# Node update of a two-layer graph network: x laid out for 6 and 8 KB pieces, one operand read from PSUM, and the pairwise additions moved to GpSimd

## The reference, cut to what matters

```
u_s  = x_s Lu_s + sum over (p, q) of Wu_ss[p, q, :] * x_s[p] * a_s[q]
                + sum over (p, q) of Wu_vv[p, q, :] * (x_v[p] . a_v[q])
u_v  = x_v Lu_v + sum over (p, q) of Wu_sv[p, q, :] * x_s[p] * a_v[q]
                + sum over (p, q) of Wu_vs[p, q, :] * x_v[p] * a_s[q]
```

## Time and profile before

| | |
|---|---|
| median of 3 runs | 14576.01 us (14514.0 to 14614.86) |
| profiled execution, its own time | 14720.34 us |
| its span | 14718.6 us |
| PE, PEld, DVE, ACT, POOL busy in the span | 75%, 52%, 58%, 33%, 57% |
| `node_update0` in the span | about 4372 to 6505 us |

### The profile page before, as it was taken

How to read it: one execution, slowest core, us unless ns; L and a number is a source line. 1 busy time by engine, 2 the same in 40 slices (tenths; PEclk the granted TensorE clock), 3 DMA queues, 4 the chain that set the end, 5 groups by cost and what they waited for, 6 DMA issues and landing times. The chain is left out here.

```text
span 14718.6 us, 198660 instructions
## 1 busy us (share of the span) xinstructions
PE 11062.6 (75%) x42082; PEld 7618.9 (52%) x42082; DVE 8564.2 (58%) x16029; ACT 4894.4 (33%) x9080; POOL 8450.8 (57%) x7876
## 2 busy tenths in 40 slices
PE   0168888888879999967787878888788787853777
PEld 0034444444432222227777777777777777741444
DVE  6316666666659999975555555555555555532332
ACT  0026666666651111112232333333323333311333
POOL 0327888788779999975554555555555555534000
PEclk9959999999989999986666666666666666655555
DMA  2127777777779999962222322223322323221000
GB/s 113 39 101 151 154 154 154 152 156 154 154 146 218 218 220 219 219 147 77 86 86 84 89 88 88 87 85 90 89 85 88 89 86 90 89 61 39 13 13 13
DMA packets 1237597, 1650.64 MB, mean 112 GB/s; under 512 B 215337, under 2 KB 865917, under 8 KB 1207261
## 3 DMA queue, kind: packets, MB, share of 16 engines
q1 hardware_dynamic: 841700, 1188.34, 29.6%
q0 software_dynamic: 395520, 458.93, 17.8%
HBM read 1472.37 MB, written 443.97 MB: 130 GB/s over the span
## 5 line engine op out<-in xcount | busy, mean ns | idle before, releaser
L461 POOL DMA_INDIRECT sums<-e_total,e_place x1568 | 2483.3, 1584 | 460.1 <-issue 419.0
L1842 POOL DMA_INDIRECT e_rows<-TS,e_at x1568 | 1624.7, 1036 | 464.1 <-issue 420.9
L1842 POOL DMA_INDIRECT e_rows<-TD,e_at x1568 | 1511.0, 964 | 477.6 <-issue 477.6
L2012 PE MATMUL ps<-e_val,e_q 128*128 128x168 f32 x3136 | 1055.7, 488 | 828.0 <-DVE e_val L1915 516.6
L2026 PEld LDWEIGHTS ps<-w_lv,e_dT 128*128 128x128 f32 x9408 | 1571.9, 245 | 0.0
L2026 PE MATMUL ps<-w_lv,e_dT 128*128 128x32 f32 x9408 | 1525.4, 306 | 0.0
L1897 DVE TENSOR_TENSOR e_silu<-e_silu,w_ad 128x256 f32<-128x256 f32 x392 | 166.6, 425 | 2315.2 <-ACT e_val L2120 1971.3
L598 PE MATMUL ps<-e_win,e_pick 128*128 128x448 f32 x3136 | 1348.4, 576 | 204.4 <-DVE e_u L495 152.9
L129 POOL TENSOR_TENSOR e_gather_cell<-zeros 1x1 f32<-1x1 f32 x392 | 186.2, 475 | 2244.4 <-DVE e_m L1854 2114.6
L2012 PEld LDWEIGHTS ps<-e_val,e_q 128*128 128x128 f32 x3136 | 803.2, 314 | 973.7 <-issue 932.3
L1990 PE MATMUL ps<-w_r,e_h 65*128 65x224 f32 x3136 | 1149.7, 537 | 129.0 <-issue 59.8
(11 more groups left out here) (392 smaller groups left out, 21971.2 us busy)
## 6 DMA issues: line engine op xcount, KB each, us to landing
e_win<-T SPq DMA_DIRECT2D x1568, 168.0 KB
n_z<-in_x_columns SPq DMA_DIRECT2D x400, 512.0 KB
n_zv<-in_x_columns SPq DMA_DIRECT2D x800, 192.0 KB
TOT<-e_tot SPq DMA_DIRECT2D x392, 352.0 KB
e_row<-in_src_rows SPq DMA_DIRECT2D x98, 1024.0 KB
e_row<-in_dst_rows SPq DMA_DIRECT2D x98, 1024.0 KB
e_win<-T SPq DMA_DIRECT2D x1568, 56.0 KB
e_local<-LR SPq DMA_DIRECT2D x98, 512.0 KB
```

The source lines that it names most:

```text
L461: pool.indirect_dma_start(sums[c], bass.IndirectOffsetOnAxis(ap=place[:, p, c:c + 1], axis=0), total[:, p, c, 0:MSG0], None, compute_op=AL ...
L1842: pool.indirect_dma_start(rows[:, p, x, c, :], None, table, bass.IndirectOffsetOnAxis(ap=at[:, gp, x, col:col + 1], axis=0)).then_inc(rows ...
L2012: last = pe.matmul(tot2[:, c % 2], q[:, j % 2, c, :], val[:, slot // 4, 4 * (slot % 4) + c, :], start=True, stop=True)
```

## The change

It does four things, all in `node_update0` and in what the host hands over:

1. The host adds two arrays with the values of x in another order: `in_x_scalar_rows` (four rows of 512 side by side) and `in_x_vector_rows` (the three components of one vector side by side). `z` is then loaded in pieces of 8 KB, `zv` and `xst` in pieces of 6 KB. The bytes are the same.
2. `scalars` on VectorE reads the stacked sums from PSUM bank A1 in place of `a0`. `a0` keeps 64 partitions. Since A1 is in use to the end of a group, `stack0` and `keep0` of the next group go to the end of the group (step 7), and the three `stack1` all use bank A0.
3. `pair` goes from VectorE to GpSimd, behind `vectors` of the same part. `p2` gets a second buffer and `mixed` no longer waits for `paired`.
4. `zv` has two buffers in place of four; `load_zv` goes to the end of SyncE's step, behind `load_x`, `load_sums` and `store`.

```diff
-        four, agT, a0 = sb("n1_four", [128, GW]), sb("n1_agT", [V3, GW]), sb("n1_a0", [128, 2, GW])
-        z, zv = sb("n1_z", [128, 4, 4, GW]), sb("n1_zv", [128, 4, 3, GW])
-        p1, p2 = sb("n1_p1", [128, 2, 3, GW]), sb("n1_p2", [128, 3, GW])
+        four, agT, a0 = sb("n1_four", [128, GW]), sb("n1_agT", [V3, GW]), sb("n1_a0", [S, 2, GW])
+        z, zv = sb("n1_z", [128, 4, 4, GW]), sb("n1_zv", [128, 2, 3, GW])
+        p1, p2 = sb("n1_p1", [128, 2, 3, GW]), sb("n1_p2", [128, 2, 3, GW])
...
                     for j in range(2):
-                        sp.dma_start(z[S * j:S * j + S, s % 4],
-                                     xT[8 * s + j:8 * s + 8:2, at].unsqueeze(0).broadcast_to([S, 4, GW])
+                        sp.dma_start(z[S * j:S * j + S, s % 4].rearrange("v k n -> v (k n)"),
+                                     xz[at, s, j].rearrange("g k n -> g (k n)").broadcast_to([S, 4 * GW])
                                      ).then_inc(z_here[s % 4], 16)
...
                 def load_zv(g, s):
-                    if not (g.before(1) and s < 4):
+                    if not (g.before(1) and s < 2):
                         gate(sp, k)
-                        sp.wait_ge(zv_used, g.n(8, s - 3))
+                        sp.wait_ge(zv_used, g.n(8, s - 1))
...
                         if ahead[0].within():
                             load_z(*ahead)
-                            load_zv(*ahead)
                         if s == 1 and g.plus(1).within():
                             load_x(g.plus(1))
                         if s == 3 and g.plus(2).within():
                             load_sums(g.plus(2))
                         if s >= 6 and not g.before(1):
                             store(g.plus(-1), s - 6)
+                        if ahead[0].within():
+                            load_zv(*ahead)
...
+                def pair(g, s):
+
+                    gate(pool, k)
+                    pool.wait_ge(weighed, g.n(16, 2 * s + 2))
+                    pool.tensor_tensor(p1[:, s % 2], p1[:, s % 2], p2[:, s % 2], ALU.add).then_inc(paired, 1)
+
                 def body(g):
                     for s in range(PARTS):
                         vectors(g, s)
+                        pair(g, s)
...
-                    dve.tensor_tensor(z[:, s % 4], z[:, s % 4], bc(a0[:, g.p, :], 4, 1), ALU.mult).then_inc(z_ready, 1)
+                    dve.tensor_tensor(z[:, s % 4], z[:, s % 4], bc(ps[:, A1, :], 4, 1), ALU.mult).then_inc(z_ready, 1)
...
                     dve.wait_ge(g_up, g.n(16, 2 * s + 2))
-                    if not (g.before(1) and s == 0):
-                        gate(dve, k)
-                        dve.wait_ge(paired, g.n(8, s))
-                    dve.tensor_tensor(p2[:], bc(ps[:, G2, :], 3, 1), xst[:, g.p], ALU.mult).then_inc(weighed, 1)
-
-                def pair(g, s):
-                    gate(dve, k)
-                    dve.wait_ge(weighed, g.n(16, 2 * s + 2))
-                    dve.tensor_tensor(p1[:, s % 2], p1[:, s % 2], p2[:], ALU.add).then_inc(paired, 1)
+                    dve.tensor_tensor(p2[:, s % 2], bc(ps[:, G2, :], 3, 1), xst[:, g.p], ALU.mult).then_inc(weighed, 1)
...
                 def stack0(g):
                     gate(pe, k)
                     pe.wait_ge(ag_kept, g.n(1, 1))
+                    if not g.before(1):
+                        gate(pe, k)
+                        pe.wait_ge(z_ready, g.n(8))
                     pe.matmul(ps[:, A1, :], W["stack"][:], agT[:], start=True, stop=True).then_inc(a0_up, 1)
...
-                            if s == 3:
+                            if s in (3, 4, 5):
+                                stack1(b, s - 3)
+                            if s == 7:
                                 stack0(b)
-                                stack1(b, 0)
-                            if s in (4, 5):
-                                stack1(b, s - 3)
                         pick(g, s)
```

More of the change, by code:

```diff
@@ L971, in groups, with node_update0 @@
         body(Group(0, 0).plus(i))
-def node_update0(nc, m, k, ps, W, xT, sums, X1, TS, TD):
+def node_update0(nc, m, k, ps, W, xT, xz, xw, sums, X1, TS, TD):
     own = ExitStack()
@@ L992, in node_update0 @@
         x_here, ag_here = [sem(f"n1_x_here{p}") for p in range(2)], sem("n1_ag_here")
-        z_here, zv_here = ([sem(f"n1_{n}_here{b}") for b in range(4)] for n in ("z", "zv"))
+        z_here, zv_here = ([sem(f"n1_{n}_here{b}") for b in range(count)] for n, count in (("z", 4), ("zv", 2)))
         stored = [sem(f"n1_stored{r}") for r in range(2)]
@@ L1100, in vectors @@
                 def vectors(g, s):
-                    b = s % 4
+                    b = s % 2
                     gate(pool, k)
-                    pool.wait_ge(zv_here[b], g.n(128, 64 * (s // 4) + 64))
+                    pool.wait_ge(zv_here[b], g.n(256, 64 * (s // 2) + 64))
                     if s == 0:
@@ L1203, in body @@
                             norm2(c)
-                        pair(g, s)
                         if s + 1 < PARTS:
@@ L1245, in stack1 @@
                         e = slice(R * j, R * j + R)
-                        last = pe.transpose(ps[:, (A0, A1, A0)[i], e], four[:, e], I[:])
+                        last = pe.transpose(ps[:, A0, e], four[:, e], I[:])
                     last.then_inc(a1_up, 1)
@@ L1263, in maps @@
                         pe.wait_ge(weighed, g.n(16, 2 * s))
-                    pe.matmul(ps[:, G2, :], W["uvs"][:, 128 * s:128 * s + 128], a0[0:S, g.p, :], start=True, stop=True
+                    pe.matmul(ps[:, G2, :], W["uvs"][:, 128 * s:128 * s + 128], a0[:, g.p, :], start=True, stop=True
                               ).then_inc(g_up, 1)
@@ L1284, in outer @@
                     pe.wait_ge(zv_ready, g.n(24, 3 * s + 3))
-                    pe.matmul(ps[0:S, U0, :], W["uvv"][:, s, :], zv[:, s % 4, 0, :], start=False, stop=s == 7
+                    pe.matmul(ps[0:S, U0, :], W["uvv"][:, s, :], zv[:, s % 2, 0, :], start=False, stop=s == 7
                               ).then_inc(zv_used, 1)
@@ L1375, in _ @@
                 turn(start)
-                stack0(start)
                 for i in range(3):
                     stack1(start, i)
+                stack0(start)
                 maps(start, 0)
@@ L1516, in body @@
                     if b.within():
-                        keep0(b)
                         keep1(b, 0)
@@ L1531, in body @@
                         keep_rows(c, 1)
+                    if b.within():
+                        keep0(b)
                 act.preload_act_table_set("natural_log_exp_and_others")
@@ L1536, in _ @@
                 copy4(start, 0)
-                keep0(start)
                 for i in range(3):
@@ L1541, in _ @@
                         copy4(start, i + 1)
+                keep0(start)
                 groups(act, body)
@@ L2645, with program @@
 ROWS = N + R
-def program(nc, x, xT, rows_src, dstC, beforeC, lower, index, rows_dst, heads_dst, first, ends, runs, ea3, ea4, ea64, nodevec, ranks, places,
+def program(nc, x, xT, xz, xw, rows_src, dstC, beforeC, lower, index, rows_dst, heads_dst, first, ends, runs, ea3, ea4, ea64, nodevec, ranks, places,
             spread_in, w, out):
@@ L2687, in program @@
                 layer0_edges(nc, m1, k, ps, W, T0, index, rows_src, LR, baseI, nodes, attr, sums0, ea64, H)
-            node_update0(nc, m0, k, ps, W, xT, sums0, X1, TS, TD)
+            node_update0(nc, m0, k, ps, W, xT, xz, xw, sums0, X1, TS, TD)
         with ExitStack() as c0:
```

28 lines of the change are left out of this document (13 added, 15 removed).

## The result

The changed kernel takes 14662.26 us (median of 6 runs, 14651.08 to 14684.52), the kernel before in the same series 14573.64 us (6 runs, 14514.0 to 14614.86). The ratio is 1.0064 [1.0043, 1.0084]. The forecast was 14656 us. The total is right and its parts are not: the stage became 193 us longer where 80 were forecast, and another stage, which was said to be untouched, became some 60 to 85 us shorter.

A forecast was written before the change was run, and what follows sets the result against it. GpSimd, by its own work plus DVE's exclusion, was the limit at 84.04 us a group; 82.3 + 2.3 + 2.2 + 0.4 = 87.2, 3.2 more times 25 is 80 us, from 14576 to 14656; range 14545 to 14780.

The forecast's parts named there:

- z product from PSUM: In the node update, the eight z products per group leave the exclusion with GpSimd, at 2.27 us each on DVE.
- the rival that its first operand keeps it in: z product stays in the exclusion because its first operand comes from SBUF: 400 us more, about 15000; chance 0.04.
- pair to GpSimd: The addition takes 3.4 us on GpSimd (3.8 kept as alternative), making its part 9.6 us, which replaces 9.42.
- GpSimd's own work: GpSimd's sum per group: eight parts of 9.6 us, 76.8, and `add_up` 5.54, together 82.3 us.
- The new wait: GpSimd waits for DVE's `mixed` in part 1, which stands behind `centre1`: 2.2 us a group.
- What stays in the exclusion: `norm1` and `norm2` still read two SBUF operands and hold up GpSimd: 2.3 us a group, bounds 0 and 2.7.
- the rival of late zv: With two buffers, part 5's zv comes 3.4 us late a group, 85 us: 14741; chance 0.13 together with clock at upper bound.
- The clock: TensorE stands some 6 us a group behind `add_up`, then runs at a lower clock: 0.4 us a group, bounds 0 and 1.9.
- In most parts there is room [...] Not in part 1: `mixed` is done some 5.6 us after its release, GpSimd needs it 9.6 us after; only part 1 waits.
- Nothing for it: Moving `stack0` and `keep0` to the group's end costs no time, as they run during GpSimd's addition or TensorE's wait.
- Nothing outside it is touched, so only this stage can change the time: Only the edited stage, 2133 us or a seventh of the launch, can change the total.
- the DMA share: Larger pieces go at 215 to 401 GB/s, gaining no time; a share still at 1 would show the forecast wrong.

The follow-up runs named there:

- warm_late: warm with `centre1` of part 1 placed behind `mixed` on VectorE; 0.9973 of the kernel before, 85.25 us a group.
- psum_pieces: Kernel before with edits 1 and 2 only (four zv buffers, old load order, addition on VectorE); 0.9903 of the kernel before, node update 2098.4 us.
- pair_order: Kernel before with edits 3 and 4 only (z product from SBUF, old 2 KB pieces); 1.026 of the kernel before, node update 2674.4 us.
- warm: Changed kernel plus six matmuls per group with unused results, ahead of TensorE's wait for part 2's zv; 1.0012 of the kernel before, 87.48 us a group.
- after_pad: Changed kernel plus 168 VectorE instructions, waits long satisfied, ahead of the node update; 1.0139 of the kernel before, edges 4600.8 us.
- after_again: Changed kernel without an edit, run on a third chip; 1.0083 of the kernel before, edges 4538.1 us.
- pieces_only: Kernel before with edit 1 only, the new arrays and pieces of 6 and 8 KB; 0.9996 of the kernel before, 84.08 us a group.

## Why the prediction was right and wrong

**Right by its steps, and the total by luck.** *z product from PSUM*: it left the exclusion in all 200 cases, and the rival that its first operand keeps it in fell. *pair to GpSimd*: 3.43 us, its 3.4. GpSimd's own work: 82.3 forecast, 81.5 found. *The new wait*: part 1 waits 2.05 us where 2.2 were derived, and warm_late, where it is gone, shows the cause that was given. *What stays in the exclusion*: 1.6 where 2.3 stood, within 0 to 2.7. GpSimd never waits for zv to land, as the forecast had it against the rival of late zv. In the edited stage alone, and added in this order, edits 1 and 2 gain 95 us (psum_pieces), edit 4 costs 129 and `pair` on GpSimd 159: 193 more in all. In another order each would have another price, as pair_order shows.

**Wrong: the step "The clock".** It said that "a few microseconds at the lower clock cost TensorE 1 to 2 us, most of which its room of about 1.5 us in part 3 covers", took 0.4 us a group and bounded it at 1.9. The cause was named rightly and its size was not: 6.3 us in a group whose clock holds, by warm, and 101 us of the stage even though warm keeps the clock in only 16 of 23 groups. What the step rested on the earlier trace rows shows a wait of 2.9 us and one window of 2 us at 0.50; it does not say when the clock came back, and "a few microseconds" was put in for that. Here it is 13 us at 1.2 GHz. And the price was counted on TensorE alone.

The timelines show the rest of the way. `second_mean` is late, `centre2` behind it starts 20.2 us after the group does where warm has 16.7, and `mixed` of part 3 stands behind `centre2` (wait of 2.46). So "In most parts there is room [...] Not in part 1" was too narrow: part 3 has `centre2` ahead of `mixed` as part 1 has `centre1`. `norm2` then starts 2.4 us after GpSimd's `pair` of part 4, and not 0.3 ahead of it as in warm, and ends behind GpSimd's next product. In VectorE's list the z product and `mixed` of part 5 follow without a gap, and `pair` waits 3.13. TensorE meanwhile waits 2.38 for that z product and reaches `stack0` late; VectorE stands 6.69 us for `keep0` before the next group's first z product, which is ahead of `mixed` of part 0 in its list (wait of 1.29; in warm it stands as long, and there is room). The forecast had said of `stack0` and `keep0` "Nothing for it".

That the three waits go with the clock is shown by warm: they are in all seven groups in which it fell and in none of the 16 others. But warm_late has those of parts 5 and 0 without the clock, from `norm2` starting with `pair`; what the clock does there is to make `norm2` late. The other links are read from the timelines, and no run broke one of them alone. DVE's busy time, 56 us a group (973.43 in 1600 us) where 50 were forecast, is the standing of `norm1` and `norm2`.

**Wrong: "Nothing outside it is touched, so only this stage can change the time".** The edges became 59 us shorter between the two profiles, and 62 or 85 in the means of all kernels, as VectorE's list ahead of their loop is 168 instructions shorter. after_pad puts the 168 back and has the old time. The stage's 193 us more less these 59 to 85 leave 108 to 134; the ratios give 93 [63, 122] in the first series and 107 [84, 130] for after_again. The forecast of +80 met the total by luck: the two errors, 113 too little in the stage and 59 to 85 too much outside, nearly cancel.

**Half wrong: the DMA share.** It fell from 1.03 to 0.87 in the middle of the stage, but only 0.05 of that is the pieces' (pieces_only). That the same bytes are spread over a longer group makes 0.90 of its 0.98 (x 84.0 / 91.8); the last 0.03 is open.

## What to carry to other kernels

Where a change opens a gap on TensorE, ask the trace how long the lower clock lasts before its price is written down, and follow the delay through every engine's list to the one that is the limit. When an edit changes the number of instructions ahead of a later loop, compare that loop's time and the packets of the instruction queue in it before the edited stage is credited with the total. And split a change: here two of its four edits gain 1%, the other two take it back, and one number for all four hides both.

## What had not been expected of the hardware

- A loop of the same code, at another place in an engine's list, was loaded anew from memory in each turn (233 packets of 8 KB in the edges, 3 where it was not), with a stall of 2.5 us a turn on VectorE and 59 to 85 us of the launch. That the packets are this code is inferred. Which places are good is not known from these runs: kernels with 2829, 2941 and 3197 instructions in VectorE's whole list had it not, those with 2997 all had it.
- The clock was 1.2 GHz for some 13 us after 6.85 us without a matmul. Over a gap of 1.6 us it stayed at 2.4 in 16 of 23 groups of one execution and fell for 6.8 us in the other seven.
- Two engines that exclude each other make small delays large: where `norm2` began 0.3 us later beside GpSimd's `pair`, it ended 3.4 us later and the group took 4.4 us more.
- 64- and 32-partition transfers kept the DMA engines busy for 1.01 of the time at 228 GB/s, 128-partition ones for 0.66 at 236, with pieces of the same size.
- One chip ran the same edges at a granted clock of 0.66, in 6200 to 6300 us, and two others at 0.88 to 0.89, in 4530 to 4610, while the node update had the same length on all three. Totals of different chips cannot be compared.
